# Attention and routed feed-forward on one core: two more unread products in the first group, and the last stage's first tile begun inside the last group

## The reference

```python
x = _layernorm(x + attn(x))      # 32 heads of 16, rope, causal softmax, plus a gated
                                 # softmax over 10 adapter keys, then w_proj
x = _layernorm(x + ffn(x))
# ffn:
base_out   = einsum('bsi,oi->bso', x, base_w) + base_b
res_hidden = einsum('bsi,ri->bsr', x, A)               # R = 64
probs      = softmax(einsum('bsi,ei->bse', x, router_w))   # E = 16
topw, topi = top_k(probs, 2);  topw = topw / (sum(topw) + 1e-6)
combine    = sum(one_hot(topi) * topw)                 # per token: weights of 16 experts
delta      = einsum('bse,bsr,eor->bso', combine, res_hidden, B)
out        = base_out + delta * 0.5
```

## Time and profile before

| | |
|---|---|
| median of 3 runs | 890.12 us (886.88 to 892.82) |
| profiled execution, its own time | 884.76 us |
| its span, first to last instruction | 882.6 us |
| mean granted TensorE clock | 0.988 |
| busy: TensorE | 860.2 us (97%) |
| busy: VectorE | 717.1 us (81%) |
| busy: ScalarE | 471.7 us (53%) |
| busy: GpSimd | 237.4 us (27%) |

### The profile page before, as it was taken

The page is one execution under the profiler, slowest core; times in us unless marked ns, Lnnn a source line. Parts: engine busy times, 40 slices in busy tenths (PEclk is TensorE's granted clock), DMA queues, the critical chain, the costliest instruction groups (busy, mean ns, idle before and its releaser), DMA issues.

```text
span 882.6 us, 15910 instructions
## 1 busy us (share of the span) xinstructions
PE 860.2 (97%) x5382; PEld 553.2 (63%) x5382; DVE 717.1 (81%) x2222; ACT 471.7 (53%) x1036; POOL 237.4 (27%) x277
## 2 busy tenths in 40 slices
PE   8999999999999999999999999999989999999996
PEld 5788868785444444444444444444468888888875
DVE  4665677689899999999999999995567777777766
ACT  4232313224688888888888888888752221212110
POOL 0222220222132333322333336332342222222221
PEclk9999999999699999999999999999999999999999
DMA  7316180737133332234342143313010010101010
GB/s 269 120 49 191 59 229 25 215 84 185 24 74 74 74 58 51 43 73 74 74 75 48 36 114 74 74 52 105 25 37 25 25 48 24 48 24 48 25 36 36
DMA packets 32338, 66.60 MB, mean 75 GB/s; under 512 B 5709, under 2 KB 7181, under 8 KB 32269
## 3 DMA queue, kind: packets, MB, share of 16 engines
q1 hardware_dynamic: 32268, 65.72, 29.2%
HBM read 44.11 MB, written 20.97 MB: 74 GB/s over the span
## 4 chain that ended last, share of the span: by engine, by line
PE 85%; DVE 6%; issue 3%; ACT 2%; DMA 2%; POOL 1%; SPq 1%; DVEq 0%; POOLq 0%
PE bank L1560 16%; PE bank L1431 15%; PE bank L422 13%; PE bank L423 12%; PE bank L424 12%; PE bank L1439 11%; PE bank L1542 2%; PE bank L1376 2%; DVE bank L1020 2%; DVE xtl L1133 1%; PE bank L1392 1%; ACT xth L874 1%; DVE mx L1023 1%; DMA y_all<-in_w_attnT 1%; DMA ks<-k_parts 1%
## 5 line engine op out<-in xcount | busy, mean ns | idle before, releaser
L849 ACT ACTIVATE pt<-bank 128x512 f32<-128x512 f32 (+3 forms) x768 | 325.6, 496 | 68.8 <-PE bank L1431 62.7
L1020 DVE CUSTOM_DVE_ANT_0 bank<-bank,cmask 128x512 f32<-128x512 f32 (+3 forms) x512 | 234.3, 526 | 10.9 <-PE bank L1439 8.1
L1431 PE MATMUL bank<-qs,ks 50*128 50x512 f32 (+3 forms) x768 | 218.3, 400 | 0.6 <-ACT pt L849 0.3
L1431 PEld LDWEIGHTS bank<-qs,ks 50*128 50x128 f32 x768 | 110.6, 186 | 139.1 <-ACT pt L849 120.4
L1023 DVE TENSOR_REDUCE mx<-bank 128x1 f32<-128x512 f32 x256 | 160.9, 687 | 10.7 <-PE bank L1439 9.4
L1560 PE MATMUL bank<-pt,vb 128*32 128x512 f32 (+3 forms) x1536 | 166.4, 506 | 0.7 <-POOL pt L671 0.7
L1439 PE MATMUL bank<-ks,qs 48*128 48x512 f32 (+3 forms) x768 | 164.1, 390 | 2.4 <-DVE mx L1020 1.4
L671 POOL TENSOR_SCALAR_AFFINE_SELECT pt<-pt 128x512 f32<-128x512 f32 x128 | 81.5, 637 | 283.8 <-ACT pt L849 283.8
L1439 PEld LDWEIGHTS bank<-ks,qs 48*128 48x128 f32 x768 | 91.8, 189 | 33.9 <-DVE mx L1020 11.3
L874 ACT CAST xth<-bank 128x512 fp32r<-128x512 f32 x16 | 9.4, 586 | 142.0 <-PE bank L1646 142.0
L614 POOL TENSOR_TENSOR part<-rope,part 128x1024 fp32r<-128x1024 f32 x16 | 38.9, 2430 | 165.2 <-ACT part L736 165.2
(11 more groups left out here) (180 smaller groups left out, 1422.4 us busy)
## 6 DMA issues: line engine op xcount, KB each, us to landing
qs<-q_parts SPq DMA_DIRECT2D x34, 256.0 KB, 4.0
ks<-k_parts SPq DMA_DIRECT2D x34, 256.0 KB, 6.8
q_parts<-part SPq DMA_DIRECT2D x32, 256.0 KB, 3.1
k_parts<-part SPq DMA_DIRECT2D x32, 256.0 KB, 3.3
qs<-q_parts SPq DMA_DIRECT2D x34, 128.0 KB, 5.0
ks<-k_parts SPq DMA_DIRECT2D x34, 128.0 KB, 5.8
vb<-in_x SPq DMA_DIRECT2D x16, 256.0 KB, 2.6
out<-outb SPq DMA_DIRECT2D x16, 256.0 KB, 2.0
```

What stands on the lines that cost most here:

```text
L849: act.activation(pt[k % PT_BUFS][:, h, 0:width(st)], half(n % SCORE_BUFS)[:, 0:width(st)], ACT.Exp, scale=float(HD) ** -0.5).then_inc(S("e ...
L1020: last = ve.tensor_tensor_reduce(blk, blk, cmask[:, BANK - nk * P:], 1.0, NEG, ALU.add, ALU.max, mx[m][:, 0, h, qt:qt + 1])
L1431: pe.matmul(half(n % SCORE_BUFS)[:, 0:q1 - q0], ks[slot_of(g)][r0:r0 + KX, h // 2, kb * P:(kb + 1) * P], qs[slot_of(g)][r0:r0 + KX, h // 2 ...
```

## The change

1. KEEP_CHUNKS becomes 3, 5, 8, 11: two more unread products of 256 columns in group 0.
2. Inside group 15 TensorE does t_x(0) at chunk 34, ar(0) at chunk 40 and t_y(2) at chunk 41; ScalarE does hi_x(0) at 34, tile_y(2) at 38, hi_y(2) at 42 and router_exp(0) at 44, each ahead of the exponential of that chunk; VectorE does arh and arl and lo_x(0) ahead of norms(1), and lo_y(2) and route(0) behind invert, all ahead of its wait for pv_done. The first tile uses other banks and buffers for this: x_bank(0) is bank 6, its parts lie in the buffer of the expanded hidden values, and router_bank(0) is bank 4.
3. t_x(1) stands ahead of the last weighted values (step 11), and proj(2) directly behind them. At j = 1 VectorE has low_b(2), lo_x(1), invert, and ScalarE hi_x(1), high_b(3), copy_out, tile_y(3).

```diff
-KEEP_CHUNKS = [3, 5]
+KEEP_CHUNKS = [3, 5, 8, 11]
...
+X_AT, ROUTER_AT, Y2_AT = 34, 40, 41
+HIGH_X_AT, ROUTER_EXP_AT, TILE_Y_AT, HIGH_Y_AT = 34, 44, 38, 42
...
+        def x_bank(t):
+            return half(FF_BANK[1] if isinstance(t, int) and t == 0 else X_BANK)
+        def router_bank(t):
+            return half(PROJ_BANK if isinstance(t, int) and t == 0 else ROUTER_BANK)
...
             def act_group(g):
...
+                    if g == G - 1 and c == HIGH_X_AT:
+                        hi_x(0, 0)
+                    if g == G - 1 and c == TILE_Y_AT:
+                        tile_y(2, 0)
+                    if g == G - 1 and c == ROUTER_EXP_AT:
+                        router_exp(0, 0)
+                    if g == G - 1 and c == HIGH_Y_AT:
+                        hi_y(2, 0)
...
             norms(0, 0)
-            norms(1, 1)
-            invert(G - 1, 0)
             ve.wait_ge(S("ar_ld"), 16)
             ve.tensor_copy(arh[:], ar_raw).then_inc(S("ar_high"), 1)
             ve.wait_ge(S("ar_high"), 1)
             ve.tensor_tensor(arl[:], ar_raw, arh[:], ALU.subtract).then_inc(S("ar_low"), 1)
+            lo_x(0, 0)
+            norms(1, 1)
+            invert(G - 1, 0)
+            lo_y(2, 0)
+            route(0, 0)
             ve.wait_ge(S("pv_done"), G * NS)
...
             def trans_out(g, i):
+                if (g, i) == (G - 1, 1):
+                    pe.wait_ge(S("x1_low"), 1)
...
             def proj(t, m, parts=range(CC)):
+                    if isinstance(t, int) and t == 2:
+                        pe.wait_ge(S("router_exp"), 1)
...
             def ar(t, m):
+                if isinstance(t, int) and t == 0:
+                    pe.wait_ge(S("attn_summed"), 2)
...
             def first_tiles(c):
+                if c == X_AT:
+                    t_x(0, 0)
+                if c == ROUTER_AT:
+                    ar(0, 0)
+                if c == Y2_AT:
+                    t_y(2, 0)
...
             for st in range(NS):
+                if st == NS - 1:
+                    t_x(1, 1)
                 if values_at(G - 1)[st] >= SCORE_BANKS:
                     weighted(G - 1, st)
+            proj(2, 0)
```

More of the change, by code:

```diff
@@ L829, in copy_out, with tile_y, hi_x, hi_g @@
                 act.copy(yrow[i][:], max_out(norm_use(g, i))).then_inc(S("out_copied"), 1)
+            def tile_y(t, m):
+                if ahead(t - 1):
+                    act.wait_ge(S("y_transposed"), t - 1)
+                bb, qt = t >> 3, t & 7
+                if not isinstance(t, int):
+                    bb = nc.s_assert_within(bb, 0, NB - 1, skip_runtime_bounds_check_because="t < NB * QT")
+                act.copy(ytile[m].rearrange("p (g n) -> p g n", g=GB),
+                         y_all[:, bass.ds(bb * GB, GB), bass.ds(qt, 1), :].rearrange("p g a n -> p g (a n)")
+                         ).then_inc(S("y_tile"), 1)
+            def hi_x(t, m):
+                act.wait_ge(S("x1_transposed"), t + 1)
+                act.copy(x_parts(t, m)[0].rearrange("p c n -> p (c n)"), x_bank(t)).then_inc(S("x1_high"), 1)
+            def hi_g(t):
+                act.wait_ge(S("g_transposed"), t + 1)
+                if isinstance(t, int) and t == NTC - 1:
+                    act.wait_ge(S("proj_full"), NTC)
+                act.copy(expanded(t)[0].rearrange("p c n -> p (c n)"), bank[0][:]).then_inc(S("g_high"), 1)
+            def router_exp(t, m):
+                act.wait_ge(S("router_neg_max"), t + 1)
+                act.copy(hr[m][:], router_bank(t)[:, 0:R]).then_inc(S("hidden"), 1)
+                act.activation(ex[m][:], router_bank(t)[:, R:R + E], ACT.Exp, bias=sm[:, 8 + 2 * m:9 + 2 * m], scale=1.0,
+                               accum_out=sm[:, 9 + 2 * m:10 + 2 * m]).then_inc(S("router_exp"), 1)
+            def hi_y(t, m):
+                act.wait_ge(S("y_transposed"), t + 1)
+                act.copy(yth[m].rearrange("p c n -> p (c n)"), half(Y_BANK)).then_inc(S("y_high"), 1)
             def act_group(g):
@@ L860, in _ @@
             evac_y(G - 1, 1)
[L862 to L890, removed]
             act.wait_ge(S("pv_done"), NS * G)
@@ L895, in act_c @@
                 sure = not isinstance(j, int)
-                if sure or 1 <= j <= NTC:
+                if not sure and j == 1:
+                    hi_x(1, 1)
+                if sure or 3 <= j <= NTC:
                     hi_x(j - 1, 1 - m)
@@ L1285, in ve_c @@
                     add_ff(j - 3, 1 - m)
-                if sure or 1 <= j <= NTC:
+                if not sure and j == 1:
+                    low_b(2)
+                    lo_x(1, 1)
+                if sure or 3 <= j <= NTC:
                     lo_x(j - 1, 1 - m)
-                if not sure and j == 1:
-                    lo_y(2, 0)
-                    low_b(2)
                 if not sure and j == 2:
@@ L1623, in proj, with t_x, ar @@
                     last.then_inc(S("proj_full"), 1)
-            def first_tiles(c):
+            def t_x(t, m):
+                pe.wait_ge(S("x1_built"), t + 1)
+                if ahead(t):
+                    pe.wait_ge(S("x1_low"), t)
+                if isinstance(t, int) and t == 1:
+                    pe.wait_ge(S("out_copied"), len(NORM) * G - 1)
+                for c_ in range(CC):
+                    last = pe.transpose(x_bank(t)[:, c_ * P:(c_ + 1) * P], x1[m][:, c_ * P:(c_ + 1) * P], ident[:])
+                last.then_inc(S("x1_transposed"), 1)
+            def ar(t, m):
+                pe.wait_ge(S("x1_low"), t + 1)
+                if ahead(t):
+                    pe.wait_ge(S("router_exp"), t)
+                if ahead(t):
+                    pe.wait_ge(S("hidden"), t)
+                if isinstance(t, int) and t == 0:
+                    pe.wait_ge(S("attn_summed"), 2)
+                if isinstance(t, int) and t == 1:
+                    pe.wait_ge(S("exp_done"), G * SCORE_BANKS)
+                pe.wait_ge(S("ar_low"), 1)
+                high, low = x_parts(t, m)
+                for c_ in range(CC):
+                    last = three(pe, router_bank(t)[:, 0:R + E], high[:, c_], low[:, c_], arh[:, c_], arl[:, c_],
+                                 c_ == 0, c_ == CC - 1)
+                last.then_inc(S("router_full"), 1)
+            def first_tiles(c):
+                if c == X_AT:
[4 more added lines that the diff above has]
+                    t_y(2, 0)
                 for t in range(2):
@@ L1658, in t_g @@
                 last.then_inc(S("g_transposed"), 1)
[L1660 to L1672, removed]
             def base(t, m):
```

28 lines of the change are left out of this document (16 added, 12 removed).

## The result

| | before | after |
|---|---|---|
| median | 890.12 us (884.99 to 892.82, 7 runs) | 883.83 us (879.76 to 889.44, 7 runs) |
| profiled execution, span | 884.76, 882.6 us | 885.01, 882.9 us |
| mean granted clock of it | 0.988 | 0.991 |

A forecast was written before the change was run, and what follows sets the result against it. TensorE, busy 97% of the span, was taken as the bound. Gains of 3.6 us in group 0 and 2.9 at the seam took the profiled 884.76 to 878.3; 5.4 up to the median gave 883.6, range 878.5 to 889.5.

The forecast's parts named there:

- its two terms: Gains of 3.6 us from the clock in group 0 and 2.9 us from last group and seam, together 6.5 us.
- the prediction's own sign: Prediction wrong if clock falls in group 0 or 15, ScalarE stands at chunk 44, or VectorE's backlog costs the gain.
- Part 1: Group 0, chunks 8 and 11: two unread products hold the clock at no cost, gaining 3.6 us until VectorE is late.
- The step that failed: Group 0: with the two products, full clock from chunk 13's to chunk 44's weighted product, 18.4 us instead of 21.94.
- Rival (b): Group 0: clock falls later or all the same, only the seam gains; -2.6 us, 887.5, chance 0.17.
- Part 2: Group 15 takes in 2.2 us of tile transposes and router product; last weighted product 2.6 us later.
- The margin at chunk 44: Group 15: VectorE's negated maximum ready 0.7 us before ScalarE's router pair needs it, so no wait was costed.
- Part 3: Seam behind group 15: 4.5 us of waits and slow clock removed; delta(0) 2.9 us earlier, counting the last group's delay.
- the new wait: Seam: TensorE waits 1.6 us before delta(0) for VectorE's lo_g(0), which stands behind route(1); bounds 0 to 2.7.
- (c): VectorE catches up in group 0 and lo_g is in time at the seam; -9.6 us, 880.5, chance 0.18.
- (d): Group 15: sparse work behind chunk 38 lowers the clock; 1.9 us slower, 892.0, chance 0.07.
- (e): Seam: the wait before delta(0) is itself followed by a clock fall, losing 1.7 us; -4.8 us, 885.3, chance 0.08.

The follow-up runs named there:

- keep_only: Original kernel plus only the two unread products at chunks 8 and 11 of group 0; 886.37 us, ratio 0.9965.
- early_g: Changed kernel with tile 0's expanded transpose and its two conversions moved ahead of tile 1's router work; 886.34 us, ratio 0.9954.
- keep30: Changed kernel plus a third unread product of 256 columns at chunk 30 of group 0; 879.71 us, ratio 0.9891.
- pairs_kept: keep30 with proj(2) put back and the last group's inserted steps moved so that no pair of scores is parted; 880.35 us, ratio 0.9882.
- keeps_no_seam: Original kernel plus unread products at chunks 8, 11 and 30, without the last-group and seam changes; 881.2 us, ratio 0.9921.
- seam_only: Changed kernel without the two added products at chunks 8 and 11, so only last group and seam differ; 888.78 us, ratio 0.997.
- pairs_kept_again: Repeat of pairs_kept, same kernel, against the original kernel; 879.89 us, ratio 0.9871.
- keep30_without_8_11: keep30 with the products at chunks 8 and 11 taken out again; 890.45 us, ratio 0.9992.

## Why the prediction was right, and where not

**The total** was 883.6 for 883.83, and that it came so close is luck: its two terms were off in opposite ways. The seam gave about half of its 2.9 us, and the clock in group 0 gave more than its 3.6, in another way than described. By the prediction's own sign (it is wrong if the clock falls in group 0) its first part failed.

**Part 1.** Two steps held: the products hide under VectorE (6.28 us from the product at chunk 3 to chunk 13's weighted product, 6.47 before, of which the last 0.57 were at half clock), and at full clock VectorE is late next (18.06 us for 18.4). The step that failed is the assumption that one added cover keeps the whole stretch. Rival (b) had it: "it falls later". In the profiled execution it fell with chunk 33's weighted product, for as long as before, and an execution without a long fall was the exception (3 of 12 in keep_only, 1 of 12 in early_g). keep30 shows the cause: with chunk 30 covered too, five executions of six had none. The gain came all the same, because the sum was made against one profiled execution at 0.988, while most executions of before are at 0.985 or less. The 5.4 us between the profiled time and the median were in front of me, and I carried them over as a constant. They are clock too: the executions of before at 0.988 and at 0.979 lie 5.8 us apart (885.3 and 891.1). Where just the fall of before goes, the profiled executions give less than the 3.6 us: 884.76 in before, 881.85 in keep_only, 2.9 us.

**Part 2** was mis-sized. The last weighted product starts 15.02 us behind score 33 (632.59 to 647.61) against 10.86 (630.74 to 641.60): 4.16 us later, for 2.6 predicted. Of the 1.6 us, 1.25 arise up to score 43: a set of transposes takes 0.59 us where I read 0.43 off the tiles of stage 3 (the trace of before has 0.59 inside group 15, too, from 633.86 to 634.45), the router product takes 1.46 for 1.37, and pairs of scores were parted, which pairs_kept gives back together with its later placing (1.03 us). The pair of ScalarE's took 0.35 us between exponentials 43 and 44 (643.94 to 644.29), near the 0.4 taken, but only half of it reached the mask: that ends 3.65 us later than before, counted from score 33 (at 647.07; before at 641.57). The rest is t_x(1): of its 0.58 us, 0.54 lie behind the mask's arrival, not inside the wait for it. The margin at chunk 44 was right: the negated maximum was ready at 643.09 (642.94 plus its 0.15) and ScalarE came at 643.94, 0.85 us for 0.7.

**Part 3** held in kind. From the last weighted product to delta(0) are 13.91 us (14.1 predicted), the new wait stands where it was put, released by lo_g(0) behind route(1), and is 1.25 us for 1.6. The clock keeps 1.00 at the seam. Its net gain (delta(0) 1.6 us earlier for 2.9) is short by what part 2 had missed. What I did not see is that proj(2) was better where it stood (0.8 us).

**The rivals.** (c) did not come: VectorE stayed the bound. (b) came in its mechanism and not in its price (887.5). (d), that the sparse work lowers the clock in group 15, is shown wrong for this kernel by the window of after over that stretch, and no trace of the other kernels with the seam changed has a fall there:

```profile
636.70:640.92 4.22, 4.22 (x34) 2.96 (x32) 2.43 (x13) 2.85 (x6) 0.71 (x1) 1.00 0.01 2
```

So here, too, the trace does not bear out a fall from transposes. The rule of the Trainium skill (TensorE: Matmul & The Clock Gate, Part 4: PE-mode transpose), that transposes do not count as work that holds the clock up, has no effect that these rows show; scores and weighted values stand between them, so they do not test it alone. (e) did not come either: the wait of 1.25 us was followed by delta(0) at 1.00.

## What to carry to other kernels

Where executions spread by a per cent, sort them by mean granted clock before reading any profile, and ask which level the profiled one stands for. A product that only holds the clock is worth most once the sparse stretches behind it are covered too, and is free where another engine sets the pace. A single profiled execution shows one of several courses of the clock, and a sum made against it holds for that course alone. Moving a product off its place uncovers the wait that it hid: ask what it covers before asking what it waits for.

## What the runs showed of the hardware

Nine falls away from the seam were profiled, and TensorE was busy nearly all through each. Six lasted about 13.7 us, wherever they lay: 13.80 us, 13.58, 13.70, 13.80, 14.00 and 13.60 in after, early_g, keeps_no_seam, seam_only and pairs_kept_again. Three did not: the short one of early_g (3.4 us), the second of seam_only (9.60) and that of keep30_without_8_11 (44.40). So a fall has no fixed length. The stretches ahead of two of them had TensorE busy 3.18 of 3.40 us and 2.71 of 3.04, and one of 2.91 of 3.24 in keep30 kept the clock.

At half clock half of the work is done, so by TensorE's own work a fall of 13.7 us costs 6.8 us, an estimate. Pairs of profiled executions with and without one give less: 2.9 us (before, keep_only), 5.1 (after, keep30) and 4.4 (pairs_kept_again, pairs_kept). It costs least in the stretch in which VectorE would be the next to be late.

In the seven executions of the changed kernel, span times (1 - clock) runs from 2.6 to 13.3 us, and a straight line in it gives each of their times to about 0.3 us, with a slope of 0.92. That is nearly all of the spread.
